# Twelve tiles a layer gathered row by row on SyncE, eleven more on ScalarE, and adjacency and degree work placed earlier

## The reference, cut to what matters

```
W = einsum('rb,bio->rio', coeff[l], basis[l])              # 8 relations
agg = segment_sum(all_h[etype, src] * norm, dst)           # relational layers, l = 0 and 1
h = relu(agg + bias)                                       # no relu after the second
x1 = layernorm(x + h)
h = x1 @ W_in + b_in
agg = segment_sum(h[src], dst) / max(deg, 1)               # three times
h = relu(agg @ W_agg[l] + h @ W_self[l] + b_hid[l])
out = layernorm(x1 + h @ W_out + b_out)
```

## Time and profile before

| what | value |
|---|---|
| median of 3 runs | 1932.81 us (1932.6 to 1933.46) |
| span of the profiled execution | 1935.5 us, 2.7 us over that median |
| PE / POOL busy over the span | 86% / 64% |
| DVE / ACT busy | 60% / 25% |
| mean granted TensorE clock | 0.963 of 2.4 GHz |

### The profile page before, as it was taken

How to read it: one execution, slowest core, us unless ns; L and a number is a source line. 1 busy time by engine, 2 the same in 40 slices (tenths; PEclk the granted TensorE clock), 3 DMA queues, 4 the chain that set the end, 5 groups by cost and what they waited for, 6 DMA issues and landing times.

```text
span 1935.5 us, 36034 instructions
## 1 busy us (share of the span) xinstructions
PE 1657.1 (86%) x9643; PEld 1378.2 (71%) x9643; DVE 1168.4 (60%) x4021; ACT 487.5 (25%) x1018; POOL 1243.6 (64%) x1311
## 2 busy tenths in 40 slices
PE   5787787887777778888899898888989999999997
PEld 3676666676566667676777787777777887777775
DVE  7978856656565656566777676775555563322344
ACT  2002111111211111122322222232455113433322
POOL 6777777777777777777777777777777773000011
PEclk9889999889999999999999999999999899999999
DMA  7344444444444444444444444445555442310011
GB/s 266 107 112 119 116 117 116 121 116 117 119 118 115 121 116 116 113 137 124 132 125 133 131 127 127 131 132 140 163 167 152 118 136 60 85 44 1 12 42 44
DMA packets 147633, 222.02 MB, mean 115 GB/s; under 512 B 81009, under 2 KB 103298, under 8 KB 147428
## 3 DMA queue, kind: packets, MB, share of 16 engines
q0 software_dynamic: 61344, 167.21, 30.4%
q1 hardware_dynamic: 49988, 38.78, 7.0%
q10 hardware_dynamic: 36096, 13.70, 2.6%
HBM read 202.31 MB, written 17.27 MB: 113 GB/s over the span
## 4 chain that ended last, share of the span: by engine, by line
PE 53%; DMA 31%; POOL 7%; issue 4%; DVE 3%; ACT 1%; DVEq 0%; ACTq 0%; POOLq 0%
PE bank L1037 21%; DMA RY<-in_x,si 19%; DMA RY<-H,si 12%; PE bank L1281 9%; PE bank L885 9%; POOL RY L352 7%; PE bank L935 3%; PE bank L1247 2%; PE bank L1291 2%; PE bank L868 1%; PE bank L1353 1%; PE bank L1002 1%; PE bank L852 1%; PE bank L950 1%; PE bank L908 1%
## 5 line engine op out<-in xcount | busy, mean ns | idle before, releaser
L1037 PE MATMUL bank<-RY 128*128 128x128 f32 x5104 | 768.9, 291 | 221.3 <-DMA RY<-in_x,si 146.8
L1037 PEld LDWEIGHTS bank<-RY 128*128 128x128 f32 x5104 | 678.9, 199 | 324.4 <-DMA RY<-in_x,si 187.7
L352 POOL DMA_INDIRECT RY<-in_x,si x638 | 611.2, 958 | 198.1 <-issue 136.9
L352 POOL DMA_INDIRECT RY<-H,si x623 | 595.0, 955 | 190.1 <-issue 138.4
L631 DVE TENSOR_SCALAR RY<-iot,c,wgt 128x128 f32<-128x128 f32 x1290 | 455.7, 358 | 389.3 <-PE bank L1037 388.2
L720 ACT CAST RY<-bank 128x320 uint8<-128x320 f32 x215 | 91.6, 426 | 684.2 <-PE bank L868 672.9
L509 DVE TENSOR_SCALAR RY<-iotN,bcol 128x320 bf16<-128x320 f16 x645 | 209.1, 324 | 0.0
L1281 PE MATMUL bank<-Ar,hs 125*128 125x500 f32 x800 | 203.9, 405 | 0.0
L623 DVE TENSOR_TENSOR RY<-RY,bank 128x256 f32 x430 | 178.4, 415 | 24.5 <-issue 13.0
L885 PE MATMUL bank<-RX,RY 128*128 128x256 f32 x704 | 189.1, 397 | 3.0 <-issue 1.8
L1342 POOL TENSOR_TENSOR x1b<-x1b,bo 125x256 f32<-125x256 f32 x20 | 14.8, 741 | 272.7 <-DMA x1b<-X 272.7
(11 more groups left out here) (148 smaller groups left out, 1311.3 us busy)
## 6 DMA issues: line engine op xcount, KB each, us to landing
ei<-in_x SPq DMA_DIRECT2D x896, 1.0 KB
ei<-H SPq DMA_DIRECT2D x896, 1.0 KB
RY<-in_x,si POOLq DMA_INDIRECT x638
RY<-H,si POOLq DMA_INDIRECT x623
Ad<-RY ACTq DMA_DIRECT2D x215, 40.0 KB
A<-Ad SPq DMA_DIRECT2D x22, 312.5 KB, 3.3
D<-Ad SPq DMA_DIRECT2D x20, 305.2 KB
RX<-in_basis ACTq DMA_DIRECT2D x2, 2048.0 KB, 21.7
```

The source lines that it names most:

```text
L352: e.indirect_dma_start(G[0:k, slot, :], None, table, bass.IndirectOffsetOnAxis(ap=index[0:k, t:t + 1], axis=0)).then_inc(s_land[slot], 16)
L1037: mm = e.matmul(bank[2 + wg % 3][:, c * 128:(c + 1) * 128], rows, S[0:k, n % NSS, :], start=(i == 0 and not ahead), stop=(i == TA - 1))
```

## The change

Per layer, SyncE fetches twelve tiles by rows instead of seven: 64, 115, ..., 625, one every 51 tiles (`SP_TILES`). ScalarE fetches seven tiles by rows in layer 0 and four in layer 1 (`ACT_SPANS`, each with its begin and its tile), with its own two buffers GA, which overlay di. GpSimd is left with 1255 gathers instead of 1276. Addresses are loaded 16 at a time on both engines. The adjacency counts come every 1.25 tiles with no break, so that they end at layer 1's tile 250. The degree loads go to tiles 262, 269, ... (every 7), the degree matmuls to tiles from 270 on (every 1.4), `pe_columns` to tile 416, and six of the eight `pe_own` calls to 420, 424, 428, 432, 490, 494.

```diff
-ROW_TILES = [96 + 84 * j for j in range(7)]
+SP_TILES = [64 + 51 * j for j in range(12)]
+ACT_SPANS = ([(16, 102)] + [(90 + 82 * j, 184 + 82 * j) for j in range(6)], [(24, 150), (138, 262), (410, 500), (488, 585)])
+ACT_TILES = [tile for spans in ACT_SPANS for _, tile in spans]
+ROW_AT = 16
...
-        while a < T and n >= 90 + a * 1.5:
+        while a < T and n >= 90 + a * 1.25:
...
-        if n == T - 1:
-            while a < 375:
-                plan.setdefault("between", []).append(a)
-                a += 1
...
-def row_plan():
+def row_plan(spans):
...
-        lo, hi = (ROW_TILES[j - 1] - ROW_LEAD if j else 2), tile - ROW_LEAD
+    for j, (begin, tile) in enumerate(spans):
         for r in range(128):
-            plan.setdefault(lo + r * (hi - lo) // 128, []).append((j, r))
+            plan.setdefault(begin + r * (tile - ROW_LEAD - begin) // 128, []).append((j, r))
...
-D_LOAD = {418 + 6 * q: q for q in range(JB)}
+D_LOAD = {262 + 7 * q: q for q in range(JB)}
 D_BLOCK = {}
 for b_ in range(NC * JB):
-    D_BLOCK.setdefault(426 + 6 * b_ // 5, []).append(b_)
-D_SUM = {451 + 24 * c: c for c in range(NC)}
+    D_BLOCK.setdefault(270 + 7 * b_ // 5, []).append(b_)
+D_SUM = {300 + 28 * c: c for c in range(NC)}
...
-OWN_TILES = (551, 555, 559, 563, 567, 571, 623, 628)
+OWN_TILES = (420, 424, 428, 432, 490, 494, 623, 628)
...
+                act_rows(e, l, t)
                 for g, k in STEPS[l].get(t, []):
                     act_post(e, l, g, k)
...
+        def act_rows(e, l, t):
+
+            table = bytes_of(x if l == 0 else H1)
+            for j, r in ACT_ROWS[l].get(t, []):
+                q = ACT_FIRST[l] + j
+                if q + r == 0:
+                    e.wait_ge(s_at, 1)
+                if l == 1 and j + r == 0:
+                    e.wait_ge(s_h1, 16 * NW)
+                if r == 0 and q > 1:
+                    e.wait_ge(s_sum, (T if q - 2 >= ACT_FIRST[1] else 0) + ACT_TILES[q - 2] + 1)
+                if r % ROW_AT == 0:
+                    act_at[:] = row_addresses(len(SP_TILES) + q, r, mybir.EngineType.Activation)
+                e.dma_start(GA8[r:r + 1, q % 2, :], table[0:1, bass.ds(act_at[r % ROW_AT], 4 * D)]).then_inc(s_rowA[q % 2], 16)
```

More of the change, by code:

```diff
@@ L34 @@
 NG = 16
-ROW_TILES = [96 + 84 * j for j in range(7)]
+SP_TILES = [64 + 51 * j for j in range(12)]
+ACT_SPANS = ([(16, 102)] + [(90 + 82 * j, 184 + 82 * j) for j in range(6)], [(24, 150), (138, 262), (410, 500), (488, 585)])
+ACT_TILES = [tile for spans in ACT_SPANS for _, tile in spans]
+ACT_FIRST = (0, len(ACT_SPANS[0]))
+BY_ROWS = {l * T + tile for l in range(2) for tile in SP_TILES + [tile for _, tile in ACT_SPANS[l]]}
 ROW_LEAD = 12
-ROW_PARTS = range((len(ROW_TILES) + 3) // 4)
+ROW_AT = 16
 NSL = 8
@@ L109 @@
 LASTG = len(GROUPS) - 1
-ROWS = row_plan()
-POOLED = [n for n in range(2 * T) if n % T not in ROW_TILES]
+SP_ROWS = row_plan([(SP_TILES[j - 1] - ROW_LEAD if j else 2, tile) for j, tile in enumerate(SP_TILES)])
+ACT_ROWS = [row_plan(spans) for spans in ACT_SPANS]
+POOLED = [n for n in range(2 * T) if n not in BY_ROWS]
 PLACE = {n: p for p, n in enumerate(POOLED)}
@@ L156 @@
 BLOCKS = {block_of(gi, c, i): (gi, c, i) for gi in range(LASTG + 1) for c in range(NC) for i in range(len(GROUPS[gi]))}
+UNIT_TILE = {unit_of(gi_, c_, mo_): t_ for t_, us in UNITS.items() for gi_, c_, mo_ in us}
 BLOCKS_AT = {}
@@ L553, in dve_unit @@
                 e.wait_ge(s_acc, q - 2 * NC + 1)
-                if gi > 7 and c < 3:
+                if c < 4 and UNIT_TILE[q] > OWN_TILES[2 * c + mo]:
                     e.wait_ge(s_owns, 2 * c + mo + 1)
@@ L647, in dve_layer @@
                     dve_select(e, l * T + u)
[L648 to L651, removed]
+                if l == 0 and t == 8:
+                    e.wait_ge(s_ix, 16)
+                    e.tensor_scalar(row_at, row_at, 4 * D, None, ALU.mult).then_inc(s_at, 1)
                 if l == 0 and t == 600:
@@ L1036, in pe_sums_of @@
                             e.wait_ge(s_row[q % 2], 16 * 128 * (q // 2 + 1))
+                    else:
+                        q = ACT_TILES.index(n - l * T, ACT_FIRST[l])
+                        rows = GA[:, q % 2, c * 128:(c + 1) * 128]
+                        if c == 0:
+                            e.wait_ge(s_rowA[q % 2], 16 * 128 * (q // 2 + 1))
                     mm = e.matmul(bank[2 + wg % 3][:, c * 128:(c + 1) * 128], rows,
@@ L1112, in sp_indices, with row_addresses @@
         def sp_indices(e):
-            for i in ROW_PARTS:
-                e.dma_start(di[32 * i:32 * i + 1, 0:512], src_rows[i:i + 1, :]).then_inc(s_ix, 16)
+            e.dma_start(row_at, src_rows).then_inc(s_ix, 16)
         def bytes_of(table):
             return table.bitcast(U8).rearrange("(o n) f -> o (n f)", o=1)
+        def row_addresses(row, r, engine):
+            _, values = nc.values_load_multi_w_load_instructions(
+                ei[row:row + 1, 512 + r:512 + r + ROW_AT], engines=[engine], min_val=0, max_val=(N - 1) * 4 * D,
+                skip_runtime_bounds_check_because="indices are numbers of rows of the table")
+            return values
+        sp_at, act_at = [], []
         def sp_rows(e, l, t):
-            table = bytes_of(x if l == 0 else H1)
-            for j, r in ROWS.get(t, []):
-                q = l * len(ROW_TILES) + j
+            table, many = bytes_of(x if l == 0 else H1), len(SP_TILES)
+            for j, r in SP_ROWS.get(t, []):
+                q = l * many + j
                 if l == 0 and j + r == 0:
@@ L1828, in _ @@
                 pe_layer(e, 0)
-                for a in COUNTS["between"]:
-                    pe_counts(e, a)
                 pe_layer(e, 1)
@@ L1840, in _ @@
                 act_layer(e, 0)
-                for a in COUNTS["between"]:
-                    act_counts(e, a)
                 act_layer(e, 1)
@@ L1853, in _ @@
                 dve_layer(e, 0)
-                for a in COUNTS["between"]:
-                    dve_counts(e, a)
                 dve_layer(e, 1)
```

36 lines of the change are left out of this document (16 added, 20 removed).

## The result

The changed kernel takes 1928.41 us, the median of 7 runs (1925.29 to 1931.67); the kernel before took 1932.81 us beside it, also the median of 7 (1932.6 to 1934.39). The ratio is 0.9973 [0.9963, 0.9984]. I had forecast 1920.5. The profiled execution of the changed kernel is the slowest of its seven, 1931.67 us with a span of 1929.9, so small differences between its trace and another are to be read with 3 us of doubt.

The account below looks back on a forecast made before the run. GpSimd's gather pace was taken to bound the kernel, followed by TensorE's lag and a final stage. The span, 1935.5 - 26.5 - 3.0 + 17.5 = 1923.5 us, gave a time of 1920.5 us, range 1901 to 1929.

Parts of the forecast that it names:

- ScalarE's rows in layer 0: Layer 0: ScalarE needs 1.14 to 1.32 us per tile against GpSimd's 1.223; the lower taken, so hidden at no cost.
- lag at the last gather: End of layer 1: columns and six own terms leave tiles 548 to 571, so TensorE lags 3 us less.
- stall in the degree stretch: Layer 1, tiles 340 to 440: late SyncE plus columns overfill the ring; GpSimd stands still 17.5 us (6.0 to 22.2).
- Fewer gathers: Both layers: 21 gathers leave GpSimd at 1.26 us each, saving 26.5 us if GpSimd never waits.
- the step that decides: SyncE's rows at 0.411 us each: it barely keeps up elsewhere but falls 22.6 us late in layer 1's degree stretch.
- SyncE isn't late: Rival, chance 0.31: the register load hides the degree load's hold, or 16 addresses cost hardly more than 8; 1903.5 us.
- the register load's floor: Alternative for SyncE's rows: with some 600 ns floor, sixteen values take about 0.97 us, stall about 10, some 1913 us.
- nothing gained: Rival, chance 0.10: lateness costs more than booked or transfers bound the gathers; stall equals the saving, 1927 to 1936 us.
- ScalarE becomes the bound in layer 0: Rival, chance 0.09: 1.32 us per tile, 55 us over, of which ring and count slack take 18; 1957 us.
- The rival's middle case: Within ScalarE's rival, layer 0: a row at the middle of the bounds gives about 1938 us.
- The counts: Until layer 1's tile 250: 0.13 more counts per tile, under 0.1 us on VectorE, less on TensorE; hidden behind GpSimd.
- 7 us from the last gather: Sign at the kernel's end: 7 us from the last gather to TensorE's last L1037, with 3 to 5 tiles of lag.

Follow-up runs that it names:

- e13: The changed kernel with the 20 degree loads issued by ScalarE instead of SyncE: 1911.93 us, ratio 0.9893 to the kernel before.
- e14: The changed kernel with the degree loads on ScalarE and five instead of seven ScalarE row tiles in layer 0: 1911.64 us, ratio 0.988.
- e17: The changed kernel with the columns and six own terms back at tiles 549 to 571 of layer 1: 1921.11 us, ratio 0.9926.
- e18: The changed kernel with degree loads on ScalarE, five ScalarE tiles in layer 0, columns and six own terms at tiles 549 to 571: 1912.06 us, ratio 0.9871.
- e15: The changed kernel with nine row tiles a layer on SyncE instead of twelve: 1913.75 us, ratio 0.9905.
- e16: The changed kernel with seven row tiles a layer on SyncE and five on ScalarE in layer 0: 1925.67 us, ratio 0.9952.
- e1 to e12: Earlier runs of the kernel before, the changed kernel and edits of both; the kernel before took 2270.55 to 2273.79 us beside them.
- e12: The kernel before, unchanged, profiled in the slower condition: 2273.6 us.
- e9: The changed kernel again, unedited, in the slower condition: 2470.07 us, ratio 1.0878 to the kernel before.
- e11: The changed kernel with SyncE's twelve tiles a layer and no rows on ScalarE, in the slower condition: 2453.27 us, ratio 1.0799.

## Why the prediction was wrong

The direction was right, the size not: a gain of 4.4 us for 12.3. The step that failed is the one that booked ScalarE's rows in layer 0 as hidden, at 0 us; they cost 7. A smaller part is the lag at the last gather, 1.5 us for 3.0. The sum, term by term:

| term | forecast | measured |
|---|---|---|
| 21 gathers fewer | -26.5 us | -26.3 (median start to start 1.251) |
| lag at the last gather | -3.0 | -1.5 (10.2 to 8.7) |
| stall in the degree stretch | +17.5 | +16.8 (timeline), 16.5 (e13) |
| ScalarE's rows in layer 0 | 0 | +7 (overrun, 14.3 against 7.2 before and 7.7 in e14) |

On the span of before the measured terms make 1935.5 - 26.3 - 1.5 + 16.8 + 7 = 1931.5 us for a span of 1929.9. What this sum doesn't explain is e14, where the 7 us are gone from layer 0 and only 0.3 (medians) to 2.5 (ratios) of them are seen at the end.

- **Fewer gathers** was right.
- **SyncE's rows, "the step that decides"**, held in place, mechanism and size. The register load of 16 values took 1.248 us (forecast 1.35), a row with its share of it 0.407 (0.411), a degree load 1.47 in the mean with the hold of the rows behind it (1.56), and the stretch 184.0 us (185.6 forecast, for one tile less):

```profile
L1127 SPq TENSOR_LOAD <-ei x192: 972/1248/1454, 36.9 to 1580.6; - x192
```

- "GpSimd stands still for 17.5 us" was tested from both sides: without the lateness 16.5 us come back, without the columns 9. The rival that SyncE isn't late (1903.5 us) falls, and with it the time by the register load's floor: the Trainium skill, page "DMA: Bandwidth & Descriptors", section "Latency and other measured facts", gives a floor of some 600 ns for a register load. Before the change one value took 282 ns on ScalarE and 442 on SyncE, eight took 786 on SyncE, and after it sixteen took 1248: some 50 to 70 ns for each further value and no such floor.
- The rival *nothing gained* names 1927 to 1936 us, and 1928.4 lies in it, but its mechanism isn't what happened: the stall is 16.8 us and not the whole saving of 29.5, and the gathers keep their 1.251 us start to start beside 21 more row tiles, so the transfers don't bound them. The number fits because a cost that it doesn't name was added. Its DMA share of at most 0.61 holds for the stretch with gathers from 50 us on; the first 50 us are at 0.76.
- **"ScalarE's rows ... hidden" is the step that failed.** The row term held: 0.63 us per tile for 0.64. The other term, "with register loads, issues and the denser counts I take 0.5", was too small. It had no row behind it: 25% is the mean of the whole span, and in layer 0 the kernel before has ScalarE busy for 16% (108.5 us from 120 to 800), 0.20 us per tile. Most of the term is queue time that no busy share holds, and the rows make that dearer. One full cycle of three counts, in ScalarE's timeline at 403 us. The view puts the last cast down to a matmul (L873), but that one ends at 407.5, and ScalarE's own register load, which starts at 407.35, takes the queue until 408.2:

```profile
403.66 0.42 ACT L724 CAST RY<-bank 128x320 uint8<-128x320 f32 x1 [3.54 <-DMA Ad<-RY]
404.30 0.39 ACTq L728 DMA_DIRECT2D Ad<-RY  x1
404.78 2.54 ACTq L1162 DMA_DIRECT2D di<-in_x  x7
408.26 0.42 ACT L724 CAST RY<-bank 128x320 uint8<-128x320 f32 x1 [4.18 <-PE bank L873]
```

  From cast to cast are 4.60 us. The seven rows are 7 x 0.324 of it, so the own part is 2.33, or 0.62 per tile at 3.75 tiles a cycle. At the average of 5.85 rows a cycle, 0.324 + 1.316 / 16 = 0.406 us each, rows and own part are 2.38 + 2.33 = 4.71 us, 1.25 per tile, where GpSimd passes a tile in 1.22; a group's work comes on top, so this excess of 0.03 is an estimate from one cycle, and a low one. It is under the 0.053 from which the rival "ScalarE becomes the bound in layer 0" makes the kernel slower. So the truth lay between forecast and rival, and I had taken the two as either-or. The rival's middle case didn't say it either: a row at the middle of the bounds, 0.47 us, makes 1.23 per tile, an excess of 0.01 or 6 us, which its own allowance of 18 us swallows; 1938 is only the mean of 1920.5 and 1957. And that allowance is too large: 0.03 x 570 = 17 us would have fitted into it whole, while in the trace the lag grows by 9 tiles, 11 us, up to 520 us and GpSimd waits from 545 us on. Why the allowance is smaller isn't tested.
- **"3 us less lag at the last gather"** was half there. From the last gather to the last matmul it is 10.2 us before, 9.7 in e17 and 8.1 in e18, with the columns late; with the columns early it is 8.7 in the changed kernel, 8.4 in e14, 6.7 in e13, 5.7 in e15 and 5.0 in e16. So moving the columns does go with a shorter end, 2.4 us in the means, but one execution can be off by as much.
- **The counts** were hidden on VectorE and TensorE, as said (e14, e16 and e18 have a lag of 3 to 4 tiles at 520 us), not on ScalarE's queue, where they are part of the step that failed. The moved matmuls are hidden where no queue is late (e13, e16).
- Of the signs that were named, the gaps between tiles 340 and 440, the register load and the degree casts waiting for their loads (66.4 us, 17 times) were there; SyncE waits for nothing at its stores in that stretch, as was said. "7 us from the last gather" wasn't, and gaps in layer 0, the sign of ScalarE's case, stood there as well.

What stays open: why e1 to e12 ran in another condition; and whether a saving of 7 us in layer 0 is kept to the end, which e14 doesn't show. That the clock at the columns decides it is read from one execution each and not tested; e18, with the columns late, doesn't show the saving either.

## What to carry to other kernels

A queue that issues many small DMAs has a budget per step of the pace-maker; work it out with everything that it issues, and don't take it from the engine's busy share. Here SyncE at 59.9 of 62.7 us and ScalarE at 1.14 of 1.22 us per tile both looked like "keeps up" with 4% and 7% to spare, and both fell behind: SyncE when degree loads came onto the same queue, ScalarE because its own part was 0.12 us dearer. Nine tiles on SyncE beat twelve by 14.7 us. Where two lumps lean on the same ring, as a late queue and the columns here, moving one away gives back half of the stall or more (9 us for the columns, 16.5 for the queue), so try first the move that costs a line.

## What the runs showed of the hardware that I had not expected

- **Small DMAs make their neighbours on the same queue dearer.** ScalarE's load of one value went from 282 ns (median) before to 570, and its issue of a 128-partition DMA from 343 to 390:

```profile
L426 ACTq TENSOR_LOAD <-ba2i x215: 282/570/792, 120.7 to 1116.6; - x108
...
L728 ACTq DMA_DIRECT2D Ad<-RY x215: 338/390/414, 127.0 to 1119.2; - x108
...
L1162 ACTq DMA_DIRECT2D di<-in_x x896: 234/235/581, 36.7 to 746.7; - x180
```

  The register load takes 572 ns right behind a row (186 of them) and 297 elsewhere (51), and the first row behind such a DMA takes 0.47 us (median of 174) instead of 0.235. Per three counts that is 0.29 + 0.05 + 0.24 = 0.58 us which no row before showed.
- **The hold behind a large load stays with a row queue.** Right behind a degree load the next row takes 0.5 to 2.2 us (median 1.2 of 18) instead of 0.228, though the load's own issue is 0.28. In the other two cases a register load stands between, and the row behind it takes under 0.3: there the hold was covered, as the rival "SyncE isn't late" had it for all of them.
- **The same kernel, 1933 or 2271 us.** In e12 GpSimd has 136 instructions between 700 and 900 us where it had 159, and its gathers waited 249 us for something outside this core's named queues:

```profile
700.00:900.00 200.00, 145.38 (x823) 122.72 (x821) 97.48 (x400) 28.81 (x60) 128.39 (x136) 0.85 0.35 100
```

```profile
  remote: 249.1, 175
```

  A gather itself takes as long as before (949 ns for 947). SyncE's instructions, whatever they are, stand in stretches of some us about 0.70 us apart: intervals of 0.65 to 0.75 us between two starts add up to 595 us in e12 and 695 in e9, and to 3.5 in the kernel before at 1933 us. In such a condition the same change is 8.8% slower (e9), of which twelve tiles on SyncE alone make 8.0% (e11), and at 1933 us it is 0.3% faster: a queue without reserve turns a small gain into a large loss. What makes the condition isn't known.
